# Where the copy of x into y is issued, and which PSUM tile the expert weights are broadcast through

## What is computed

```python
def _hgrn_forward(x, Wi, Wf, Wg, g_norm_weight, Wo):
    i = jnp.einsum('bld,ed->ble', x, Wi)
    f = jnp.einsum('bld,ed->ble', x, Wf)
    gate = jax.nn.sigmoid(f)
    i_in = jax.nn.silu(i) * (1.0 - gate)
    _, o = jax.lax.associative_scan(combine, (gate, i_in), axis=1)
    g = jnp.einsum('bld,ed->ble', x, Wg)
    rms = jax.lax.rsqrt(jnp.mean(jnp.square(g), axis=-1, keepdims=True) + EPS)
    out = g * rms * g_norm_weight * (o * jax.nn.sigmoid(o))
    return jnp.einsum('ble,de->bld', out, Wo)
...
x = x + _hgrn_forward(_layernorm(x), Wi, Wf, Wg, g_norm_weight, Wo)
# the feed-forward part: 8 experts of 1024, the best 2 of each token, router_w on _layernorm(x)
gate = silu(einsum('nd,edf->enf', xf, w1)); value = einsum('nd,edf->enf', xf, w2)
expert_out = einsum('enf,efd->end', gate * value, w3)
x = x + sum over the 2 chosen experts of topk_weights * expert_out
```

## Time and profile before

| | us |
|---|---|
| two runs shown | 4452.84 and 4736.37 |
| their median | 4594.61 |
| the profiled execution | 4353.97 |
| its span, slowest core (2) | 4352.1 |
| spans of the eight cores | 4329.4 to 4352.1 |
| PE busy | 3752.6 |
| mean granted clock of PE, core 2 (all cores) | 0.951 (0.951 to 0.954) of full speed |
| DVE busy | 1334.3 |
| ACT busy | 398.4 |

### The profile page before, as it was taken

The page is one execution under the profiler, slowest core; times in us unless marked ns, Lnnn a source line. Parts: engine busy times, 40 slices in busy tenths (PEclk is TensorE's granted clock), DMA queues, the critical chain, the costliest instruction groups (busy, mean ns, idle before and its releaser), DMA issues.

```text
span 4352.1 us, 43266 instructions; the slowest of 8 cores (4329.4 to 4352.1 us)
## 1 busy us (share of the span) xinstructions
PE 3752.6 (86%) x18483; PEld 1777.0 (41%) x18832; DVE 1334.3 (31%) x1138; ACT 398.4 (9%) x379; POOL 323.8 (7%) x360
## 2 busy tenths in 40 slices
PE   0199799998962499999999999999999999999992
PEld 0055444443431244444444444444444444444442
DVE  0522255553225522322322322222232232232231
ACT  0322121210004000000000000000000000000000
POOL 0000000000001000100000010010010010010011
PEclk9999899999985699999999999999999999999995
DMA  9411211201249233344343344343343343343239
GB/s 158 160 35 35 49 35 34 39 11 25 36 72 160 28 34 39 34 42 42 30 42 38 34 42 39 32 40 37 35 43 39 30 39 39 34 44 39 22 34 155
DMA packets 416236, 212.61 MB, mean 49 GB/s; under 512 B 399392, under 2 KB 399392, under 8 KB 409648
## 3 DMA queue, kind: packets, MB, share of 16 engines
q0 software_dynamic: 413296, 176.22, 34.7%
q1 hardware_dynamic: 2752, 33.61, 3.3%
HBM read 318.89 MB, written 50.33 MB: 85 GB/s over the span
## 4 chain that ended last, share of the span: by engine, by line
PE 79%; DVE 8%; DMA 6%; another core or an unknown queue 3%; issue 2%; ACT 2%; DVEq 0%; POOL 0%; ACTq 0%; POOLq 0%; SPq 0%
PE pga L827 21%; PE pw L888 20%; PE pva L842 20%; PE po L571 5%; PE pg L332 5%; PE pi L473 3%; PE pf L473 3%; DMA y<-fsc 2%; DMA y<-gvw 2%; DVE fsc L505 2%; DMA fsc<-x 1%; DVE bufB L513 1%; DVE fsc L512 1%; DVE bufA L257 1%
## 5 line engine op out<-in xcount | busy, mean ns | idle before, releaser
L827 PE MATMUL pga<-bufA,wsc 128*128 128x512 bf16 x4012 | 912.5, 383 | 5.0 <-issue 0.7
L888 PE MATMUL pw<-gvw,wsc 128*128 128x512 bf16 x4015 | 894.8, 383 | 24.5 <-DVE gvw L861 19.1
L842 PE MATMUL pva<-bufA,wsc 128*128 128x512 bf16 x4014 | 899.8, 379 | 4.3
L888 PEld LDWEIGHTS pw<-gvw,wsc 128*128 128x128 bf16 x4096 | 403.2, 99 | 516.2 <-issue 44.1
L827 PEld LDWEIGHTS pga<-bufA,wsc 128*128 128x128 bf16 x4096 | 403.5, 99 | 495.3 <-issue 22.1
L842 PEld LDWEIGHTS pva<-bufA,wsc 128*128 128x128 bf16 x4096 | 400.7, 98 | 483.4
L762 POOL DMA_DIRECT2D wsc<-w x256 | 258.6, 1012 | 2511.4 <-PE pga L827 1196.9
L900 DVE TENSOR_TENSOR bufB<-pw,bufB 128x1024 bf16<-128x1024 f32 x224 | 274.3, 1225 | 524.2 <-PE pw L888 524.2
L854 DVE TENSOR_TENSOR gvw<-fsc,pga 128x1024 bf16<-128x1024 f32 x128 | 156.3, 1221 | 795.7 <-ACT fsc L850 795.7
L850 ACT ACTIVATE fsc<-pga 128x1024 f32<-128x1024 f32 x128 | 131.1, 1024 | 2499.4 <-PE pga L827 2499.4
L858 DVE TENSOR_TENSOR scr<-pva,fsc 128x1024 bf16<-128x1024 f32 x128 | 156.7, 1225 | 577.3 <-PE pva L842 577.3
(11 more groups left out here) (112 smaller groups left out, 1406.8 us busy)
## 6 DMA issues: line engine op xcount, KB each, us to landing
wsc<-w POOLq DMA_DIRECT2D x128, 512.0 KB, 6.7
wsc<-w POOLq DMA_DIRECT2D x128, 256.0 KB, 4.5
fsc<-x SPq DMA_DIRECT2D x16, 1024.0 KB, 5.5
y<-fsc POOLq DMA_DIRECT2D x16, 1024.0 KB, 10.0
y<-gvw POOLq DMA_DIRECT2D x16, 1024.0 KB, 11.0
wsc<-wg POOLq DMA_DIRECT2D x16, 512.0 KB, 5.1
wsc<-wo POOLq DMA_DIRECT2D x16, 512.0 KB, 5.1
gvw<-wi POOLq DMA_DIRECT2D x16, 512.0 KB, 5.1
```

Of the source, the lines that this page charges most:

```text
L827: ins = e.matmul(out=pga[:, n2 * 512:(n2 + 1) * 512], lhsT=lhsT, rhs=bufA[:, k * 2048 + nn:k * 2048 + nn + 512], start=(k == 0), stop=(k = ...
L842: ins = e.matmul(out=pva[:, n2 * 512:(n2 + 1) * 512], lhsT=lhsT, rhs=bufA[:, k * 2048 + nn:k * 2048 + nn + 512], start=(k == 0), stop=(k = ...
L888: ins = e.matmul(out=pws[_sl][:, n2 * 512:(n2 + 1) * 512], lhsT=lhsT, rhs=gvw[:, k * 2048 + nn:k * 2048 + nn + 512], start=(k == 0), stop= ...
```

## The change

The copy of x into y is taken from its place ahead of the x loads and issued behind them on the same queue. The broadcast of the expert weights uses pw0 for the first half of the tokens and pw1 for the second; each half waits for and records the release of its own accumulator, and the reader of the weights waits for the second copy as before.

```diff
--- before.py
+++ after.py
@@ -184,8 +184,6 @@
         misc_load("sync", lambda e: e.dma_start(out=selsb[:], in_=sel_dram.ap()))
-        ypre.n += 16
-        on("sync", lambda e, _h=ypre.h: e.dma_start(out=yout, in_=xin).then_inc(_h, 16))
         MISC_S = miscs.n
@@ -206,6 +204,8 @@
             xs.release(slot, [(ve, v), (ac, ac.n)])
         AC_STAGE1 = ac.n
         VE_STAGE1 = ve.n
+        ypre.n += 16
+        on("sync", lambda e, _h=ypre.h: e.dma_start(out=yout, in_=xin).then_inc(_h, 16))
@@ -783,13 +783,13 @@
                 for hb in range(2):
-                    if pw_rel[0] is not None:
-                        wait("tensor", ve, pw_rel[0])
+                    if pw_rel[hb] is not None:
+                        wait("tensor", ve, pw_rel[hb])
                     def bc(e, _e=e_, _hb=hb):
                         ins = None
                         for n2 in range(2):
-                            ins = e.matmul(out=pw0[:, n2 * 512:(n2 + 1) * 512],
+                            ins = e.matmul(out=pws[_hb][:, n2 * 512:(n2 + 1) * 512],
                                            lhsT=selsb[:, _e * 128:(_e + 1) * 128],
@@ -797,9 +797,9 @@
                     wait("vector", te, v_b)
-                    pw_rel[0] = emit("vector", lambda e, _hb=hb: e.tensor_copy(
-                        out=wb_ap[:, _hb * 1024:_hb * 1024 + 1024], in_=pw0[:]), inc=ve)
-                v_wb = pw_rel[0]
+                    pw_rel[hb] = emit("vector", lambda e, _hb=hb: e.tensor_copy(
+                        out=wb_ap[:, _hb * 1024:_hb * 1024 + 1024], in_=pws[_hb][:]), inc=ve)
+                v_wb = pw_rel[1]
```

## The result

The changed kernel takes 0.9793 of the time before, with an interval of 0.9775 to 0.981, so it is faster, by 1.9 to 2.25%. The median over all its 11 runs is 4315.68 us, with the lowest at 4259.95; before, 4499.15 and 4351.16 over 10 runs. The ratio leaves out the runs in which one half of the chip had a lower granted clock, which is why it says more than the medians. The profiled execution took 4270.81 us. My figures were 4273 us and a ratio of 0.981, and I gave the outcome "within 2%" the largest chance, 0.59. The time came out close to the forecast. The measured ratio lies on the other side of my 2% border, which its interval contains, so the runs do not settle on which side the kernel is. Inside the sum four terms were off, in both directions, so part of the agreement in time is luck.

The account below looks back on a forecast made before the run. Mostly PE matmuls bound the kernel, except an opening where x loads wait behind the copy. -108 (x earlier) +36.3 (block 2 wait) +2.1 (restart) -10.9 (broadcast) = -80.5 us, giving 4273 us, ratio 0.981; range 4225 to 4515.

Parts of the forecast that it names:

- Part 2: Two accumulators for the experts' weight broadcast (line 792): PE's waits on DVE's copy shrink by 10.9 us, bounds 8 to 17.9.
- the landing of block 2: Opening, POOL's queue: wg block 2, loaded beside the copy, lands 60.6 us after its issue, as block 0 did before.
- instruction fetch: PE's instructions also come by DMA beside the copy; one turn of 7.15 us per packet was held too short to stop PE.
- What bounded the opening: Opening, SP's queue: x loads stand behind the y<-x copy, which takes 114.4 us to land; DVE and PE wait for x.
- Shift of stage 1: x loads and DVE's squares: moving the copy brings them forward 108 us (112.9 less 5 for POOL's opening loads), bounds 96 to 114.
- PE's wait for block 2: Between the halves of m=1, PE stands 36.3 us for wg block 2, slowed by the copy; bounds 33, 47, or 0.
- The restart at half speed: After the wait for wg block 2, PE restarts at near 1.2 instead of 2.4 GHz, costing 2.1 us; bounds 0 and 5.
- the main case: Whole kernel: the summed forecast, 4273 us with its own range 4255 to 4300; chance 0.72.
- rival B: Opening: PE's instruction packets also wait on the copy; in the extreme transposes start at 188.5 us, total 4328 us; chance 0.07.
- A: Opening: loads share the DMA engines finely, so PE neither waits for wg block 2 nor restarts; 4235 us, chance 0.15.
- C: Whole kernel: PE's granted clock drops from its 0.951 mean, 39.5 us per 0.01; 4376 us at 0.925; chance 0.04.
- D: Opening: the x loads are slow by themselves, not held by the copy; only the broadcast gains, 4343 us; chance 0.02.

Follow-up runs that it names:

- e5: e3 with POOL's first transfers (gwt, wg blocks 0 and 1) held until DVE is done with x tile 13; ratio 0.9728 to the kernel before.
- e2: The kernel before with only the two accumulators for the broadcast, the copy staying ahead of the x loads; ratio 0.9956 to the kernel before.
- e3: The changed kernel with the copy issued as two transfers of half rows, in 4 KB pieces; ratio 0.9733 to the kernel before.
- e10: The changed kernel with the copy issued as two transfers in pieces of 32 KB instead of 64 KB; ratio 0.9771 to the kernel before.
- e6: e3 with an expert's first w3 group waiting only for its own half of the product; ratio 0.9659 to the kernel before.
- e1: The kernel before with only the copy moved behind the x loads, the broadcast staying in pw0; ratio 0.9842 to the kernel before.

## Why the prediction was right or wrong

The mechanisms of the large terms held. Two steps of the sum failed in size, and both made the gain larger than forecast. Part 2 was priced at the waits alone, 10.9 us, where a half-speed stretch behind each 2.34 us gap came on top: 22.5 us on core 2. And the landing of block 2 was put at 60.6 us, where it took 50.4, so that wait and restart cost 28.2 us in the g stage and not 38.4. Two smaller costs, the x stage and the instruction fetch, took some of it back.

**What bounded the opening: right.** The x loads stood behind the copy, and the changed order brought them forward at once.

**Shift of stage 1, 108 us: 102.9 on core 2.** What was mis-sized here is the 5 us for what runs beside the x loads. The first tile came at 9.6 instead of 8.5, and the 15 tiles behind it took 8.9 us more than 61.3. e5 takes those transfers away and gets 8.2 and 59.7. Of my bound (0 to 16.9) the middle would have been the better choice.

**PE's wait for block 2: the place and the mechanism right, 25.0 us instead of 36.3.** The turns are nearly as I described, 6.8 us each instead of 7.15, with a delay of 7.6 us before the first. But I took 60.6 us for the landing, though only six turns were left: block 2 is issued 61.7 us behind the copy (133.91 against 72.2), not 53, because the last x tile lands late and the transposes stop once, and the copy landed 111.8 us after its issue instead of the 119.5 I counted; no run separates why. The load then finished with the end of the copy, after 50.4 us. My bounds of 33 and 47 took the landing from rows of one overlap and did not move it with the other terms. The restart at half speed was forecast at 2.1 us; the rows 1.86 against 1.06 and 8.19 against 7.07 make it 1.9.

**Instruction fetch: left at zero in the main case, 5.64 us on core 2.** I had put it down as rival B in its extreme, and dismissed it by the rate of the g stage. PE takes instructions two and a half times as fast in short transposes (32, with the weight loads, in 1.33 us) as in matmuls of 512 columns (some 128 in 13.98 us), and it is among the transposes that it stopped, when the packet came 11 us later behind the first transpose than before the change.

**Part 2: 10.9 us forecast, 22.5 measured on core 2, 19.5 in the mean.** This is the largest miss in proportion. The waits were right to 0.1 us. What I left out is that PE's gap of 2.34 us was followed by a half-speed stretch, and the stretch 1859 to 1862 before the change, shown with e2, has it: clock 0.54, and 9 matmuls where e2 has 15. I had used the same effect at PE's restart and not asked whether it holds at a short gap.

**The sum.** On core 2: 102.9 - 6.8 - 28.2 + 2.4 + 22.5 + 0.8 = 93.6 us instead of 80.5. The gain beyond forecast comes from part 2 and the shorter wait; the opening and the stop on issue gave some of it back. The profiled execution gained 83.2 us only, since its slowest core is core 7, which ends 10.5 us behind core 2: 2.5 us of that are there at the first transpose (its 15 tiles took 71.2 us), 5.1 come in the experts' stretch, where it has two half-speed stretches more, and 3.8 behind it. By the ratio the gain is about 90 us. I had put the border of 2% six us away from my value, and the errors left over were about that large.

**Rivals.** A fell, by the 25 us wait and by e3 and e10. B's mechanism was there, with 5.64 us where its extreme had some 92 (188.5 less 95.9). C fell: the mean clock is 0.949 to 0.951. D fell with the first x load, which landed after 7.3 us.

## What to carry to other kernels

A transfer that nobody waits for is not free: here it delayed what was queued behind it in full, and what ran on another queue by one turn per row, each turn about as long as one of its pieces. Issue it behind what the opening needs, and in small pieces; here 4 KB pieces were worth 25 us and cost nothing that showed. A gap of PE of 2.3 us cost 1.7 us more than itself here (half of the 3.4 us at half speed behind it), so look at the granted clock behind a gap before you price it, behind short ones too, and look for waits that ask for more than the waiting step reads: the first w3 group waited for a half that it did not use, and that was worth as much as the whole wait for the weights.

## What the runs showed of the hardware that I had not expected

- Beside a copy with 64 KB pieces a load's rows start 6.8 us apart on a DMA engine, 3.7 us beside 32 KB, and about 1 us beside 4 KB, while the total rate stays at 157 to 169 GB/s (from 100 us on, changed kernel and e3). Before the first row 4 to 8 us pass (block 2 of the changed kernel, e10 and e3).
- A PE gap of 2.3 to 2.7 us was followed by a half-speed stretch of 3.4 us at all 15 such gaps in the experts' stretch of core 2 before the change, and at 113 of 120 over the eight cores. Behind a gap of 1.0 us one stood in 8 of 56 places after the change, in 1 of 56 in e2, and in 22 of 56 in e6.
- PE stopped for want of instructions for up to 8.7 us (e1, core 4) while the copy inside HBM ran, in a stretch of short transposes, and on no core of the four kernels without the copy beside that stretch. The stop always stood at the same matmul and ended 0.6 to 1.6 us after an instruction packet.
